# One VectorE instruction for the one-hots of two consecutive count tiles

## What is computed

```python
# layernorm(x): zero mean and unit variance over the 512 numbers of a node
agg = segment_sum(layernorm(x)[src], dst, 2500)     # sum over the edges that end in a node
h   = relu((layernorm(x) + agg) @ W1 + b1)
x   = x + h @ W2 + b2
# mixture of 8 experts, the top two of a softmax gate for each node
x   = x + sum_e score[:, e] * (gelu(layernorm(x) @ eW1[e] + eb1[e]) @ eW2[e] + eb2[e])
```

## Time and profile before

| what | value |
|---|---|
| median of 3 runs | 621.04 us (620.58 to 622.58) |
| time of the profiled execution | 625.51 us |
| its span, first to last instruction | 623.5 us |
| TensorE busy | 552.6 us, 89% |
| VectorE busy | 467.7 us, 75% |
| GpSimd busy | 285.5 us, 46% |
| ScalarE busy | 281.8 us, 45% |
| line 1130, `hot_key` | 125 instructions, 108.3 us, mean 866 ns |
| line 1130, `hot_lo` | 125 instructions, 84.3 us, mean 674 ns |
| mean granted TensorE clock | 0.948 of full |

### The profile page before, as it was taken

One profiled execution on the slowest core, in us unless ns is written; L12 is line 12 of the kernel. 1 busy time (PEld: TensorE's weight loads), 2 busy tenths in 40 slices (PEclk: granted clock), 3 DMA queues, 4 the chain that ended last, 5 costly groups with the idle time before them and its releaser, 6 DMA issues.

```text
span 623.5 us, 13412 instructions
## 1 busy us (share of the span) xinstructions
PE 552.6 (89%) x4500; PEld 420.3 (67%) x4501; DVE 467.7 (75%) x979; ACT 281.8 (45%) x539; POOL 285.5 (46%) x237
## 2 busy tenths in 40 slices
PE   5689879999989999999999999982389999999980
PEld 3589779766657766776676665582377888888760
DVE  4777879967369999989898733269979677776773
ACT  3455657534153236233523230056158556565562
POOL 4362233202034555334642443253437777777753
PEclk9898989999799999999999999986599999999995
DMA  8252500200041333242223222396398888888775
GB/s 259 89 142 52 160 1 1 74 6 1 2 106 53 95 118 117 87 133 101 86 85 100 69 65 78 90 356 215 91 351 153 161 158 154 156 157 154 149 110 68
DMA packets 39547, 71.70 MB, mean 115 GB/s; under 512 B 12169, under 2 KB 16409, under 8 KB 38826
## 3 DMA queue, kind: packets, MB, share of 16 engines
q0 software_dynamic: 11328, 25.55, 22.4%
q1 hardware_dynamic: 21327, 31.08, 15.7%
q10 hardware_dynamic: 6834, 14.34, 7.2%
HBM read 43.46 MB, written 29.06 MB: 116 GB/s over the span
## 4 chain that ended last, share of the span: by engine, by line
PE 69%; DVE 20%; ACT 4%; issue 3%; DMA 2%; ACTq 1%; SPq 0%; POOLq 0%; DVEq 0%; PEldq 0%
PE psum L1537 23%; PE psum L1691 10%; PE psum L1681 9%; PE psum L1521 8%; PE psum L1576 7%; PE psum L1451 6%; DVE hot_key L1130 3%; DVE hot_lo L1130 3%; PE psum L1658 3%; DMA src_i<-in_src 1%; DVE stat L943 1%; PE psum L1429 1%; ACT h L746 1%; DVE ln L1155 1%; DVE x L1153 1%
## 5 line engine op out<-in xcount | busy, mean ns | idle before, releaser
L1130 DVE TENSOR_TENSOR hot_key<-iota_key,key_w 128x1200 f16<-128x1200 f16 x125 | 108.3, 866 | 29.6 <-PE psum L1521 28.6
L719 ACT ACTIVATE counts<-psum 128x400 bf16<-128x400 f32 x125 | 62.1, 507 | 142.3 <-PE psum L1521 140.9
L1537 PE MATMUL psum<-counts,z_hi 125*128 125x500 bf16 x400 | 103.0, 379 | 2.3 <-ACT h L746 1.7
L1537 PE MATMUL psum<-counts,z_lo 125*128 125x500 bf16 x400 | 101.5, 377 | 0.0
L658 POOL DMA_INDIRECT out_x<-y,target_i x47 | 75.3, 1601 | 36.6 <-issue 18.1
L1521 PE MATMUL psum<-hot_key,hot_lo 128*128 128x200 f16 x750 | 83.4, 251 | 5.0 <-DVE hot_lo L1130 3.3
L1130 DVE TENSOR_TENSOR hot_lo<-iota_lo,lo_w 128x768 f16<-128x768 f16 x125 | 84.3, 674 | 0.0
L1521 PEld LDWEIGHTS psum<-hot_key,hot_lo 128*128 128x128 f16 x750 | 66.3, 98 | 25.7 <-issue 5.6
L620 POOL TENSOR_TENSOR xt<-xt_whole,xt 125x512 f16<-125x512 f32 x20 | 50.5, 2526 | 53.9 <-DVE xt L1170 39.9
L1537 PEld LDWEIGHTS psum<-counts,z_lo 125*128 125x128 f16 x400 | 39.4, 98 | 46.0 <-issue 1.6
L902 ACT ACTIVATE he<-psum,eb_col,up_undo 128x128 f32<-128x128 f32 x94 | 42.4, 457 | 56.0 <-PE psum L1681 54.7
(11 more groups left out here) (274 smaller groups left out, 1139.1 us busy)
## 6 DMA issues: line engine op xcount, KB each, us to landing
out_x<-x SPq DMA_DIRECT2D x20, 224.0 KB
xt_d<-xt SPq DMA_DIRECT2D x20, 224.0 KB
x_res<-in_x SPq DMA_DIRECT2D x19, 224.0 KB
up_raw<-in_L_ffn_W ACTq DMA_DIRECT2D x8, 512.0 KB, 4.1
up_d<-up_split ACTq DMA_DIRECT2D x8, 512.0 KB
w_both<-up_d SPq DMA_DIRECT2D x8, 512.0 KB, 8.0
w_raw<-in_L_ffn_W SPq DMA_DIRECT2D x8, 512.0 KB, 9.3
W_raw<-in_L_gnn_W ACTq DMA_DIRECT2D x2, 1024.0 KB, 5.3
```

The lines of the kernel that those rows point to most:

```text
L719: act.activation(counts[:, it % 2, :, place:place + W], psum[:, WIN + w % 2, 0:MW].rearrange("p (w h) -> p h w", w=W), ACT.Copy).then_inc( ...
L1130: ins = dve.tensor_tensor(hot[:, w % RING].rearrange("p s (n two) -> p s n two", two=2), iota[:].rearrange("p (o n two) -> p o n two", o=1 ...
L1537: ins = mm(psum[:, AGG + c, 0:GN], half[:, t, c * 128:(c + 1) * 128], counts[0:P, g % 2, t], start=(t == 0 and n == 0), stop=(t == T - 1 a ...
```

## The change

For even w one instruction builds `hot_key` of windows w and w + 1, and one builds `hot_lo` of both; for odd w nothing is issued. `hot_ready` is raised by 2 after the second. The ring still has four places, so both places of a pair must be free: the wait is now for window w - 3 and all before it (`win_done` at w - 2) instead of window w - 4. The last window, 124, is alone. All other work keeps its place in the written order; nothing changes on the other engines.

```diff
@@ -1123,15 +1123,18 @@
             def one_hots(w):
-                if w >= RING:
-                    dve.wait_ge(S["win_done"], w - RING + 1)
+                if w % 2:
+                    return
+                n = min(2, NW - w)
+                if w + n > RING:
+                    dve.wait_ge(S["win_done"], w + n - RING)
                 for hot, iota, value, width in ((hot_key, iota_key, key_w, MH), (hot_lo, iota_lo, lo_w, 128)):
-                    shape = [128, SL, width // 2, 2]
-                    ins = dve.tensor_tensor(hot[:, w % RING].rearrange("p s (n two) -> p s n two", two=2),
+                    shape = [128, n * SL, width // 2, 2]
+                    ins = dve.tensor_tensor(hot[:, w % RING:w % RING + n].rearrange("p r s (n two) -> p (r s) n two", two=2),
                                             iota[:].rearrange("p (o n two) -> p o n two", o=1, two=2).broadcast_to(shape),
-                                            value[:, w].rearrange("p s (o two) -> p s o two", o=1).broadcast_to(shape),
+                                            value[:, w:w + n].rearrange("p r s (o two) -> p (r s) o two", o=1).broadcast_to(shape),
                                             ALU.is_equal)
-                ins.then_inc(S["hot_ready"], 1)
+                ins.then_inc(S["hot_ready"], n)
```

## The result

The median of the changed kernel is 642.52 us (641.22 to 643.95, four executions), that of the kernel before, measured beside it, 621.81 us (620.58 to 626.38, four). The ratio is 1.0324, with a 95% interval of 1.0278 to 1.037: 20.7 us slower. The profiled executions took 642.16 and 625.51 us, 16.6 us apart.

What follows compares the result with a forecast made beforehand. TensorE was taken to bound passes 2 and 3, with VectorE close behind. Waits of 13.5 us from order and GpSimd plus 3.2 us of clock gave 16.7 us, so 621.0 + 16.7 = 637.7 us, range 629 to 645 us.

Steps and rivals of the forecast that it cites:

- What a pair costs: On VectorE, a pair of windows takes 2.19 us against 2.32 now; 124 fewer instructions save 8.7 us of busy time.
- What it costs in order: In VectorE's order, pairs start later and run longer ahead of work TensorE awaits: 9.9 us without GpSimd, 13.5 with it.
- everywhere else a pair is wanted at least 2 us after it is ready: At all places not listed in passes and first layer, the pair has enough margin, so no time is added.
- The term for j = 2 of pass 3: Last residual of the group before, behind the one-hots of j = 4: the longer pair adds 1.0 us.
- First layer: At t = 12, window 8 comes some 0.5 us later and the wait before window 9 goes: +0.2 us.
- GpSimd: In passes 2 and 4, GpSimd and VectorE shut each other out for whole instructions, raising the sum from 9.9 to 13.5 us.
- Clock: TensorE's granted clock falls after two of five new idles, 1.6 us each, 3.2 us; none and five are the ends.
- second sign of being wrong: The prediction would be wrong if TensorE's clock falls after each idle; it took two falls for five idles.
- VectorE's saving coming through (1): 8.7 us less VectorE work would end TensorE's waits on it: faster, 615.9 us at best; 5%.
- The ring still covering it (2): up_sums and mlp2 have more slack than a pair costs: no change, 621 us; 6%.
- The wide instruction being slow in itself (3): On VectorE, one number a cycle in place of two: 124 us more, kernel above 700 us; 1%.
- The order without GpSimd and clock (4): Low end of its own case, 9.9 us, 631 us; high end with five falls 645 us; the case has 88%.

Runs made afterwards that it cites:

- e7: The changed kernel plus idle matmuls of 256 columns on TensorE in the five places where it waits, results never used; ratio 1.0281 to the kernel before.
- e1: The changed kernel with its order and wait, but one narrow instruction per window (four in a row in place of two); ratio 1.0488 to the kernel before.
- e12: The changed kernel run again, unaltered, on the chip of the follow-up runs as their reference; ratio 1.0339 to the kernel before.
- e2: The kernel before with only the stricter ring wait (even windows wait for one window more), order and instructions kept; ratio 1.0253 to the kernel before.
- e6: The changed kernel with every residual and up_scales moved ahead of the pair that holds its window, ring of four; ratio 0.9971 to the kernel before.
- e10: The kernel before, one instruction per window and its own wait, with residual and up_scales moved ahead; ratio 0.9968 to the kernel before.
- e3: The changed kernel with six places in the ring in place of four; ratio 1.0004 to the kernel before.
- e8: The changed kernel with light GpSimd work (h_lo set to zero, bias added to 8 of 512 columns); ratio 1.0268 to the kernel before.
- e5: The changed kernel with logits and residual ahead of the pair only at j = 4 and 14 of the even passes; ratio 1.0218 to the kernel before.

## Why the prediction was right

The forecast was 637.7 us within 629 to 645; measured were 642.5. The mechanism is the one that was forecast. Its sum was 16.7 us, 16.5 of it in passes 2 to 4, where the profiles show 22.0: the sum missed 2.3 us of waiting, 1.8 of them in pass 3, and 3.3 us of clock. The median moved by 20.7 us, 4.0 more than the sum, and stayed inside a range whose upper end had been set by five falls of the clock. How near a forecast with two falls comes depends on how many an execution happens to have, and that part of the agreement is luck. That the two profiled executions are 16.6 us apart is no confirmation: the profile of before lay 3.7 us above its median, and outside the passes the profile of the change was 5.4 us the shorter one.

| place | forecast wait, us | measured, us |
|---|---|---|
| pass 2, j = 4, `mlp2` | 2.6 | 2.29 |
| pass 2, j = 12, `up_sums` | 2.5 | 2.39 |
| pass 2, j = 14, `mlp2` | 0.65 | 0.59 |
| pass 3, j = 2, `up_sums` | 1.9 | 1.24 |
| pass 3, j = 9, `counts` | none | 0.25 |
| pass 3, j = 12, `up_sums` | 0.3 | 0.53 |
| pass 3, j = 20, `counts` and `up_abs` | none | 1.24 and 0.35 |
| pass 4, j = 2, `up_sums` | 3.9 | 3.93 |
| pass 4, j = 4, `mlp2` | 0.65 | 0.59 |
| pass 4, j = 12, `up_sums` | 2.5 | 2.39 |
| pass 4, j = 14, `mlp2` | 0.7, as before | 0.59 |

Forecast waits are the added time plus the wait of before in the place. They are counted by steps, the measured ones by brackets, which leave out some 0.16 us of each, as said above.

- *What a pair costs.* 2.19 us forecast; 2.20 at 207.32, medians 1.407 and 0.952 us against 1.40 and 0.95. VectorE's busy time fell by 10.4 us between the two profiles; 8.7 was forecast.
- *What it costs in order.* Direct time by pass, from e7, where no clock is in it: 5.6, 3.1 and 6.9 us; forecast 5.3, 1.3 and 6.7. Passes 2 and 4 are right. **The failed step is pass 3**, the term left at nothing by "everywhere else a pair is wanted at least 2 us after it is ready". That sentence counted only TensorE's use of the pair. In pass 3 the residual and `up_low` stand behind the pair (19, 20), which met GpSimd, and another engine waits for them. TensorE lost 1.24 + 0.35 us at j = 20 by that. The term for j = 2 of pass 3 was off the other way, +1.0 forecast and +0.35 measured: before, both instructions of window 79 met GpSimd (steps of 1.38 and 1.52 us), while of the pair, whose `hot_key` starts at 245.06, only `hot_lo` did (2.00 us at 246.38). VectorE, then ScalarE in the profile after:

```profile
287.43 2.29 DVE L1133 TENSOR_TENSOR hot_key<-iota_key,key_w 128x2400 f16<-128x2400 f16 x1 [1.57 <-PE psum L1524]
...
292.74 1.19 DVE L1190 TENSOR_TENSOR up_split<-up_raw,up_split 128x1024 f16<-128x1024 f32 x1
...
292.86 0.29 ACT L724 ACTIVATE ln<-ln,eps_down 125x1 f32<-125x1 f32 x1 [2.72 <-DVE ln L1159]
293.96 0.34 ACTq L776 DMA_DIRECT2D up_d<-up_split  x1
294.34 0.31 ACTq L777 DMA_DIRECT2D inverse_d<-up_inverse  x1
294.69 0.50 ACT L719 ACTIVATE counts<-psum 128x400 bf16<-128x400 f32 x1 [1.54 <-PE psum L1524]
```

  ScalarE first waits 2.72 us for the residual's statistics (the row at 292.86), then for `up_low` (292.74, done at 293.93), whose stores it issues. The copy of the counts of window j = 18 out of PSUM, made ready by TensorE at 291.8, is queued behind all this and starts at 294.69. TensorE, which needs that bank for window j = 20, waits 1.24 us for it, at 295.25. The last 1.1 us of ScalarE's waiting are in front of a DMA issue, which no busy time shows.
- *First layer*, +0.2 forecast. TensorE's wait for one-hots rose from 3.3 to 4.3 us, so some +1.0, and the stretch with its two fewer falls agrees (-2.4 + 2 x 1.63 = +0.9).
- *GpSimd*, 3.6 forecast, 2.9 measured. The Trainium skill, SBUF — State Buffer, section Who interferes with whom, calls it an exclusive lock. The rows agree: a one-hot that meets GpSimd is held up by 1.05 us where a GpSimd instruction alone takes 1.16. e1 adds that the cost grows with the number of VectorE instructions in the stretch: narrow and wide ones were held up by about as much each.
- **Clock, mis-sized.** Two falls and 3.2 us forecast; the profile had four (6.5 us), e12 two, e2 three. The price of one was right by e7. Of the six idles of over 1 us in the profile, the four of 2.29 us and more were followed by a fall, the two of 1.24 us were not; in e12, with waits of the same length, only the two of pass 4 were. What decides it is not shown. The prediction's second sign of being wrong, a fall after each idle, was nearly met: four of its five places had one.
- *Rivals.* VectorE's saving coming through (1): refuted, since even where all waits are taken away (e6 against e10) the ratios are the same. The ring still covering it (2): refuted for four places, true for six (e3). The wide instruction being slow in itself (3): refuted by its medians and by e1. The order without GpSimd and clock (4): too low, as e7 and e8 show a price for each; its upper end, 645 us with five falls, lay nearer to the measured time than the sum did.

## What to carry to other kernels

Here two steps of a producer joined in one instruction freed no time, since the consumer was the bound. Joining them cost a place of lookahead in the ring, and what stands behind them in the producer's order came later by that wait and by the second step's work: before joining, look at what else is queued behind, also what reaches the consumer through a third engine that waits to issue a DMA. If it must be joined, add the ring places or put the urgent work ahead of the pair; either took the whole cost away here, and neither made it a gain.

## What the runs showed of the hardware

- Seven of eight narrow one-hot instructions next to GpSimd in e1 were delayed by some 1.05 us each, the wide ones of the change that met it by 0.5 to 1.1 us in the places shown. A GpSimd instruction alone took 1.16 us. Splitting the pair into four instructions made the same meeting cost more: e1's `mlp2` at j = 4 waited 5.6 us against 2.3.
- Of two executions of the same kernel with the same waits, one had four falls of the granted clock in passes 2 to 4 and the other two. Length alone doesn't tell them apart: in e5 the wait of 2.18 us in pass 4 was followed by a fall and the one of 2.29 us in pass 2 wasn't. Idle matmuls in the waits removed all of them and returned 1.6 us for each, but they did not make TensorE go on sooner (15.5 us direct with them and without).
